# The add of the two rotation halves moves from GpSimd to VectorE, inside the 16 intervals

## The reference

```python
xn = layernorm(x)
Q, K, V = xn @ Wq.T + bq, xn @ Wk.T + bk, xn @ Wv.T + bv      # 16 heads of 16
Q, K = rope(Q), rope(K)          # re = xe*cos - xo*sin ; ro = xe*sin + xo*cos
attn = softmax(causal(Q @ K.T / 4)) @ V
y = square(relu(xn @ W_fc.T)) @ W_proj.T                      # width 1024 inside
spikes = five steps of a leaky integrate-and-fire cell on y, counted / 5
out = x + (attn @ Wo.T + bo) + spikes
```

## Time and profile before

| | us |
|---|---|
| median of 3 runs | 2170.7 |
| lowest, highest | 2169.31, 2172.22 |
| the profiled execution, its own time | 2166.99 |
| its span, first to last instruction | 2165.3 |
| TensorE busy | 2088.6 (96%) |
| ScalarE busy | 1444.7 (67%) |
| VectorE busy | 1385.3 (64%) |
| GpSimd busy | 1111.0 (51%) |

### The profile page before, as it was taken

One profiled execution on the slowest core, in us unless ns is written; L12 is line 12 of the kernel. 1 busy time (PEld: TensorE's weight loads), 2 busy tenths in 40 slices (PEclk: granted clock), 3 DMA queues, 4 the chain that ended last, 5 costly groups with the idle time before them and its releaser, 6 DMA issues.

```text
span 2165.3 us, 67675 instructions
## 1 busy us (share of the span) xinstructions
PE 2088.6 (96%) x25492; PEld 1510.5 (70%) x25492; DVE 1385.3 (64%) x2139; ACT 1444.7 (67%) x1676; POOL 1111.0 (51%) x1072
## 2 busy tenths in 40 slices
PE   5999999999999999999999999999999999999995
PEld 4677676777767677676777767677676777767663
DVE  7576585766758566585666758566585666757443
ACT  3666667676676767667667676767667667676662
POOL 5464463645546455464645546455463645646341
PEclk9999999999999999999999999999999999999998
DMA  5353636445364553635445364553635445364442
GB/s 200 120 165 95 186 103 170 128 120 184 93 178 119 138 168 95 193 106 158 140 120 180 93 179 120 135 172 95 195 106 155 143 120 178 91 175 126 113 115 71
DMA packets 169866, 299.97 MB, mean 139 GB/s; under 512 B 25104, under 2 KB 114960, under 8 KB 157200
## 3 DMA queue, kind: packets, MB, share of 16 engines
q1 hardware_dynamic: 169616, 296.10, 47.6%
HBM read 174.89 MB, written 103.28 MB: 128 GB/s over the span
## 4 chain that ended last, share of the span: by engine, by line
PE 81%; ACT 4%; DMA 4%; DVE 4%; issue 3%; SPq 2%; POOL 1%; ACTq 0%; DVEq 0%; POOLq 0%
PE pair L1530 22%; PE pair L1327 21%; PE pair L1513 12%; PE pair L1336 9%; PE pair L1305 7%; PE pair L1253 5%; PE pair L1319 4%; ACT probs L813 3%; SPq L441 2%; DMA recip_rows<-recip_dram 2%; DMA qk_dram<-rot_b 1%; PE pair L1271 1%; PE pair L1468 1%; DVE xn L951 1%; DVE rot_b L1004 0%
## 5 line engine op out<-in xcount | busy, mean ns | idle before, releaser
L813 ACT ACTIVATE probs<-pair 128x1024 f32<-128x1024 f32 x1152 | 1139.7, 1029 | 503.8 <-PE pair L1513 502.0
L688 POOL TENSOR_TENSOR h_lo<-h_sq,h_hi 128x512 fp32r<-128x512 f32 x256 | 409.9, 1601 | 478.0 <-DVE h_hi L1072 477.6
L1336 PE MATMUL pair<-wproj_hi,h_hi 64*128 64x256 f32 x2048 | 590.1, 288 | 0.0
L1336 PE MATMUL pair<-wproj_hi,h_lo 64*128 64x256 f32 x2048 | 572.3, 279 | 0.0
L1336 PE MATMUL pair<-wproj_lo,h_hi 64*128 64x256 f32 x2048 | 571.6, 279 | 0.0
L1327 PE MATMUL pair<-xT_hi,wfc_hi 64*128 64x256 f32 x2048 | 551.0, 288 | 6.4 <-DVE fin L1019 2.5
L696 POOL TENSOR_SCALAR_AFFINE_SELECT probs<-probs 128x512 f32<-128x512 f32 x512 | 376.4, 753 | 341.9 <-ACT probs L813 341.9
L1530 PE MATMUL pair<-probs,v_sb 128*17 128x512 f32 (+3 forms) x6144 | 545.3, 488 | 0.9 <-ACT probs L813 0.9
L1327 PE MATMUL pair<-xT_lo,wfc_hi 64*128 64x256 f32 x2048 | 536.0, 280 | 0.0
L1327 PE MATMUL pair<-xT_hi,wfc_lo 64*128 64x256 f32 x2048 | 535.2, 279 | 0.0
L1513 PE MATMUL pair<-q_ring,k_ring 64*128 64x512 f32 (+3 forms) x3072 | 442.4, 355 | 19.6 <-ACT probs L813 14.1
(11 more groups left out here) (113 smaller groups left out, 2901.8 us busy)
## 6 DMA issues: line engine op xcount, KB each, us to landing
q_ring<-qk_dram SPq DMA_DIRECT2D x384, 128.0 KB
k_ring<-qk_dram SPq DMA_DIRECT2D x384, 128.0 KB
qk_dram<-planes SPq DMA_DIRECT2D x64, 512.0 KB, 2.8
qk_dram<-rot_b SPq DMA_DIRECT2D x62, 512.0 KB, 3.8
xn<-in_x SPq DMA_DIRECT2D x16, 1024.0 KB, 5.6
rs<-in_x SPq DMA_DIRECT2D x64, 256.0 KB, 2.8
acc_dram<-rs SPq DMA_DIRECT2D x64, 256.0 KB, 2.2
attn<-numer SPq DMA_DIRECT2D x256, 64.0 KB, 2.4
```

Source lines behind the costliest of these rows:

```text
L688: pool.tensor_tensor(h_lo[i % HB][:, :], h_sq[i % HB][:, :], h_hi[i % HB][:, :].bitcast(F32), ALU.subtract).then_inc(h_lo_done, 1)
L813: act.activation(probs[BUFFER[n]][:, 2 * pr:2 * pr + 2, :], pair[m % NSLOT][:, :, :], ACT.Exp, scale=SCALE).then_inc(exp_done, 1)
L1336: return pe.matmul(proj_bank[:, t * D:(t + 1) * D], h[rows, a * T2 + t * P:a * T2 + (t + 1) * P], w[rows, f, :], start=i % ITEMS_OF_GROUP ...
```

## The change

GpSimd no longer adds the halves in the intervals. VectorE adds them itself, right behind the second half of each rotation, with a wait on `rot_done`, which is its own semaphore from the instruction just before. The opening is not changed: there GpSimd still adds, and its `sum_qk` stays for that.

```diff
@@ gpsimd, interval @@
                     if att and place == 4 and diagonals(2 * n + 1):
                         mask(b, 2 * n + 1)
-                    if more and at in SUM_QK_AT:
-                        sum_qk(nb, SUM_QK_AT[at])
                     for i in expanded.get(at, ()) if more or final else ():
                         h_low(item, i)
@@ vector, new function @@
+            def sum_qk(nb, u):
+                dve.wait_ge(rot_done, nb * 4 + u + 1)
+                dve.tensor_tensor(rot[u % 2][:, :, :], rot[u % 2][:, :, :], rot_b[u % 2][:, :, :], ALU.add).then_inc(rot_sum, 1)
@@ vector, interval @@
                         if u:
                             low_qk(nb, u - 1)
                         rotate(nb, u, 1, None)
+                        sum_qk(nb, u)
                     if last and place == 2 and n in O_AT:
                         finish(b - 1, O_AT[n])
```

## The result

| | before | after |
|---|---|---|
| median, us | 2171.46 (6 runs) | 2187.32 (6 runs) |
| lowest, highest | 2169.31, 2174.83 | 2181.1, 2189.94 |
| the profiled execution, its own time | 2166.99 | 2189.94 |
| its span | 2165.3 | 2188.2 |

The ratio of the changed kernel to the kernel before is 1.0071, 95% interval [1.0055, 1.0087]: 16 us slower.

A forecast was written before the change was run, and what follows sets the result against it. TensorE, busy 2088.6 of 2165.3 us, was taken as the bound. Shift alone gave 12.3 us, with tails 20.3; added to the profiled 2166.99 that made 2187.3, stated as 2188, range 2178 to 2193.

The forecast's parts named there:

- The add on VectorE: Four adds per interval, 60 in all, behind the rotations on VectorE, each taken as 1.22 us.
- Rival D: The add on VectorE overlaps a GpSimd mask and takes up to 1.65 us: 2194 us; chance 0.05.
- The shift d: Unit 2's add delays numerator copy, `finish` of quarter 1, ring 2 and the store of unit 2's planes by 1.25 us.
- GpSimd's relief: Removing 60 adds of 2.396 us from GpSimd gains nothing, as the masks around the sum waited for ScalarE.
- The path through `finish`, ring 2 and the planes: Unit 2's add delays `finish` of quarter 1, SyncE's ring 2 DMAs and planes store, then ScalarE and TensorE, in 14 intervals.
- A loss of w - 1.26: ScalarE's wait w for unit 2's planes costs TensorE nothing up to 1.26 us, and one for one above.
- The second term, the tails: Six more planes transfers end behind an instruction packet, adding up to 1.65 us to each wait; sum 20.3 instead of 12.3.
- The stretch from first to third `rectify`: On ScalarE, around the wait for unit 2's planes: 13.2 us in most intervals, 11.05 in none.
- A: Unit 2's planes land later by the delay alone, without new tails: 12.3 us, 2179 to 2183 us; chance 0.25.
- B: No change: instruction packets move away from the planes store altogether, +1.3 us, about 2172 us; chance 0.08.
- C: Faster: sum ready 1.18 us earlier, GpSimd freer, add hidden behind TensorE's output product at `finish`: 2166 us; chance 0.05.

The follow-up runs named there:

- the shift of TensorE's code: 128 semaphore increments ahead of everything else on TensorE: 2196.7 us on the changed kernel, 2186.78 us on the kernel before.
- the doubled delay: Changed kernel with one more 128x1024 two-input VectorE instruction ahead of unit 2's add: 2196.43 us, ratio 1.0125 to the kernel before.
- unit 2's add alone: Kernel before with only unit 2's add moved to VectorE, the other three staying on GpSimd: 2193.05 us, ratio 1.0088.

## Why the prediction was right

**The forecast** was 2188.0 us, in a range of 2178 to 2193; measured 2187.32. The path is the one that was forecast. That the time came out within 1 us is in part luck. The sum of 20.3 us stands against 17.8 in steps 7 and 8 of the profiles, 16.1 without the fall of the clock, and against 15.9 between the medians; but it was added to the profiled execution of before, 2166.99, which is 4.5 us below the median of six, and 0.7 of that was put back. The steps one by one:

- The add on VectorE: taken as 1.22 us from `low_qk`, measured 1.225 in all 60, with no spread. Rival D (it meets GpSimd, up to 1.65) found no case: GpSimd had no work beside any of the 60. The shift d was put at 1.25; the copy moved by 1.26, `finish` by 1.18. The 0.08 between them fit the wait for TensorE's product, which ended at about 886.77 and had held `finish` by that much. The planes' second issue moved by 1.21 on average.
- GpSimd's relief is worth nothing, and three of four adds are covered: shown by the kernel with all but unit 2's add moved, and by the 2171.16 us with all four moved and unit 2's behind `finish`.
- The path through `finish`, ring 2 and the planes: the chain shows the store in 13 of 14 intervals, and once in interval 0, where it doesn't come by way of `finish` (there is none) but by a tail.
- A loss of w - 1.26: the best step. In 12 of the 14 intervals wait less loss is 1.25 to 1.27 us, at waits from 1.48 to 3.85; of the other two one has the fall of the clock (1.7 more), and the last interval 1.20. The bound had come from one difference, and held to 0.01 us.
- The second term, the tails: present, but about half the size, and its reason right in part. ScalarE's wait was put at 42 us, 34 for the shift and 8 for new tails; in the 14 intervals it is 38.3, so the tails brought 4. That a packet inside the transfer makes its tail was argued from two transfers; the shift of TensorE's code bears it out with 28 short landings. What was wrong is that the packets keep their place ("repeat within 0.2 us from interval to interval"): in the profile after they start anywhere from 0.3 us before to 4.1 us after the second issue. So there are landings from 3.66 us (two intervals, where the packet came behind) to 5.84. Packets that started from 0.3 us before to 0.1 after the issue cost 0.7 to 0.8 us, those from 0.7 to 2.3 after it 1.5 to 2.2. Over the 14 intervals that is 1.2 us on average, where eleven tails of 1.65 would make 1.3; but before the change it was 0.9 already. One landing was overlooked there: the last of the 14 took 5.58 us, with its packet inside, and cost nothing then only because its store is issued 1.5 us earlier than the others.
- The stretch from first to third `rectify`, forecast as 13.2 us in most intervals and 11.05 in none, is 11.28 to 14.74, 12.65 on average. None is at 11.05; only one is within 0.2 us of 13.2.
- What no step had: TensorE's clock. TensorE's pause at a long wait was at times followed by 3.4 us at 1.2 GHz, 1.7 us each. In the change's profile it happened once in these intervals; with the doubled delay three times.
- Of the rivals, A (shift alone, 12.3 us) is as near to the medians' 15.9 as the forecast's 20.3, and two of the six runs (2181.1, 2183.67) lie in its range or just above. The profile stands between the two: the shift came in full, and about half of the second term. B and C fall with the measured sign. For C, the place where it was to decide went nearly as argued: `finish` was held by VectorE and TensorE's product at almost the same moment, so the add delayed it by 1.18 of 1.26 us.

**The rules that the prediction quoted.** The Trainium skill's sentence that a block's fetch costs one tail-bump, mostly hidden ("Runtime: NRT & Kernel Launch", section Instruction fetch mechanics), does not hold here for a store that a packet falls into and that ScalarE waits for: 3.6 to 3.9 us from the second issue to landing without a packet in it, 4.2 to 5.8 with one. The Trainium skill's rule that VectorE is the engine for such adds ("GPSIMD Engine Reference", section 4.1) is right by the durations (1.225 against 2.396 us) and said nothing on the time of this kernel: with the planes of unit 2 first in SyncE's list both places give 2162 us.

## What to carry to other kernels

An instruction moved to an idle engine is not free because the engine is idle: ask what stands behind it in that engine's list and which queue waits for that, here a 0.7 us output add, with 16 DMAs behind it on SyncE. Before moving work between engines, look at the order of the DMA queue: put a transfer whose source is ready and whose landing someone waits for ahead of the ones that can wait; that alone was worth 10 us here, and with it the two places of the add were 0.5 us apart. To size such a move, find the slack once from two instances of the same wait (wait against time lost), and count only what lies above it. Compare the sum with the difference between the kernels, and not only the time with the time: here the time agreed to 1 us and the sum was 4 us too large.

## What the runs showed of the hardware

- A 16 KB instruction packet, 0.9 to 1.7 us long at this place, delays a 1 MB store of planes that it falls into: the landings of the kernels before and after took 4.2 to 5.8 us from the second issue with a packet inside, and 3.6 to 3.7 us without. At the end such a store runs at 15 to 30 GB/s for 1.5 us; one of 16 engines would carry 22 to 25 of the 350 to 400 GB/s before it, an estimate from the same row, which is why one engine is taken to be the late one. The 28 transfers of the two kernels with shifted code, and the 28 of the two with the planes first, had no packet start between the second issue and the landing, and landed 3.59 to 3.91 us after it.
- TensorE's clock fell from 2.4 to 1.2 GHz for 3.4 us after TensorE had been busy for 1.04 of 2.5 us. Such a fall did not follow every long wait of ScalarE: in the profiles of the change, of unit 2's add alone and of the doubled delay it followed waits of 3.26, 3.24, 3.38, 3.67, 3.73, 3.92 and 4.05 us, and not those of 3.62, 3.67, 3.76 and 3.85.
- An instruction with two SBUF inputs on VectorE (`low_qk`, 1.22 us) kept its time with GpSimd's `h_low` beside it, while GpSimd's took 2.19 us instead of the 1.27 of its shortest (kernel before, from 253.53 us; VectorE's had started 0.17 us ahead). Where a mask of GpSimd had started 0.24 us ahead of it, from 122.79 us, it took 1.65.
- The two-input fp32 add of 128x1024 on VectorE took 1.224 to 1.226 us in 60 of 60 cases; GpSimd's had a median of 2.396.
